# Square sums two heads behind the queries, squares rounded straight from the bank, and weight remainders shared by GpSimd and VectorE in the stage between two layers

## The reference

```python
x = x + softmax(q k / scale) v @ Wo                      # end of layer 0's attention
x = x + einsum('btd,rde->bte', layernorm(x), factors) / sqrt(8) + bias
q = (layernorm(x) @ Wq).reshape(B, Sq, 16, 128)          # layer 1
q = q * rsqrt(mean(square(q), axis=-1) + 1e-5) * gq
```

## Time and profile before

| | us |
|---|---|
| median of three runs | 2167.49 (2165.17 to 2168.35) |
| profiled execution | 2165.27 |
| its span | 2163.5 |
| TensorE busy in the span | 2098.3 (97%) |
| VectorE, ScalarE, GpSimd busy | 1622.5, 1085.9, 1425.9 |
| granted TensorE clock, mean | 0.994 of full speed |

### The profile page before, as it was taken

One profiled execution on the slowest core, in us unless ns is written; L12 is line 12 of the kernel. 1 busy time (PEld: TensorE's weight loads), 2 busy tenths in 40 slices (PEclk: granted clock), 3 DMA queues, 4 the chain that ended last, 5 costly groups with the idle time before them and its releaser, 6 DMA issues. The chain is left out here.

```text
span 2163.5 us, 27510 instructions
## 1 busy us (share of the span) xinstructions
PE 2098.3 (97%) x8514; PEld 1522.0 (70%) x8514; DVE 1622.5 (75%) x2560; ACT 1085.9 (50%) x3408; POOL 1425.9 (66%) x1071
## 2 busy tenths in 40 slices
PE   7999999999999999999999888999999999999999
PEld 7777777777677777777777456666666666665998
DVE  4889999999999999999987642556566666652577
ACT  3565556555555565655656137444434344431433
POOL 1477787777877887778776146187878778771221
PEclk9999999999999999999999999999999999999999
DMA  3000000000000000000010410011011111101110
GB/s 132 29 15 19 26 29 16 29 15 29 29 15 15 29 29 15 22 23 29 21 43 1 147 40 1 29 43 58 29 57 38 49 53 33 43 1 52 37 52 25
DMA packets 15140, 75.64 MB, mean 35 GB/s; under 512 B 1746, under 2 KB 2114, under 8 KB 13986
## 3 DMA queue, kind: packets, MB, share of 16 engines
q1 hardware_dynamic: 14994, 73.89, 10.4%
HBM read 72.97 MB, written 0.92 MB: 34 GB/s over the span
## 5 line engine op out<-in xcount | busy, mean ns | idle before, releaser
L539 ACT ACTIVATE l_prod_act<-l_prod_act 125x128 f32<-125x128 f32 x1152 | 342.1, 299 | 354.6 <-DVE l_prod_act L714 354.5
L634 POOL TENSOR_TENSOR l_prod<-l_prod 125x256 f32<-125x256 f32 x480 | 350.3, 738 | 239.5 <-DVE l_prod L714 239.5
L968 POOL TENSOR_TENSOR l_acc<-l_acc,l_probs 125x896 f32<-125x896 f32 x160 | 346.2, 2163 | 81.5 <-ACT l_probs L918 65.8
L714 DVE TENSOR_TENSOR l_prod<-l_side,xq 125x512 f32<-125x512 f32 x480 | 324.8, 677 | 45.0 <-PE l_side L823 38.4
L988 DVE TENSOR_TENSOR l_scaled<-l_slots,rk 125x896 f32<-125x896 f32 x192 | 206.9, 1084 | 197.6 <-PE l_slots L1053 197.5
L918 ACT ACTIVATE l_probs<-l_scaled 125x896 f32<-125x896 f32 x192 | 182.9, 953 | 320.5 <-DVE l_scaled L988 298.8
L628 POOL TENSOR_TENSOR l_acc<-l_acc,l_probs 125x896 f32<-125x896 f32 x160 | 339.3, 2121 | 0.0
L557 ACT ACTIVATE l_probs<-l_slots,mask_bias 125x448 f32<-125x448 f32 x384 | 225.0, 623 | 59.8 <-PE l_slots L775 54.1
L684 DVE SCALAR_TENSOR_TENSOR top<-l_side,mask_bias,top 125x448 f32<-125x448 f32 x330 | 216.5, 664 | 7.9 <-PE l_side L806 7.9
L539 ACT ACTIVATION_READ_ACCUMULATOR l_prod_act<-l_prod_act 125x1 f32 x1152 | 217.0, 188 | 0.0
L723 DVE TENSOR_REDUCE l_msq<-l_prod 125x4 f32<-125x256 f32 x480 | 196.3, 410 | 22.4 <-POOL l_prod L634 22.4
(11 more groups left out here) (256 smaller groups left out, 4623.8 us busy)
## 6 DMA issues: line engine op xcount, KB each, us to landing
land<-in_ctxT SPq DMA_DIRECT2D x32, 750.0 KB, 4.0
l_nat<-in_ctxN SPq DMA_DIRECT2D x16, 750.0 KB
post_we<-in_experts SPq DMA_DIRECT2D x20, 384.0 KB, 3.0
spare<-in_ctxN SPq DMA_DIRECT2D x8, 750.0 KB
nat<-in_ctxN SPq DMA_DIRECT2D x8, 750.0 KB
spare<-in_wo SPq DMA_DIRECT2D x2, 2048.0 KB, 8.7
spare<-in_wqT SPq DMA_DIRECT2D x4, 512.0 KB, 9.2
mid_fac<-in_factors SPq DMA_DIRECT2D x1, 2048.0 KB, 8.0
```

What stands on the lines that cost most here:

```text
L539: last = act.activation(whole, whole, ACT.Copy, accum_out=msq[:, t, 4 * g + c:4 * g + c + 1])
L634: pool.tensor_tensor(buf[:, :, 0:C // 2], buf[:, :, 0:C // 2], buf[:, :, C // 2:C], ALU.add).then_inc(s.half_sum, 1)
L714: dve.tensor_tensor(to[:, :, :], bank, xt.unsqueeze(1).to_broadcast([KT, 4, C]), ALU.mult).then_inc(s.side_dve, 1)
L968: pool.tensor_tensor(acc[:, :], acc[:, :], P[t % NP][:, :], ALU.add).then_inc(s.acc, 1)
```

## The change

Four things are changed in `between_layers`.

1. `ms` of head n stands two heads behind the query product, with the last two sums of half 0 among the first queries of half 1; `sqh` and `sql` have three buffers.
2. ScalarE computes the rounded square from the bank a second time, with a rounded output, instead of rounding `sq`. The even heads' copies of half 0 go from ScalarE to VectorE, which copies after both squares.
3. Weight remainders of even n stay with GpSimd, those of odd n are VectorE's, with a semaphore of their own. GpSimd's bias add is done tile by tile, those of half 1 between the first four heads' squares.
4. The reciprocals of half 0 stand at heads 2 to 5 of half 1 on VectorE, and ScalarE's rounding of the inverse at head 6 instead of head 2.

```diff
...
 MID += [("t1", 0, 0), ("t1", 0, 1), ("f", 0, 0), ("f", 0, 1), ("y", 1, 1), ("t2", 0, 0), ("t2", 0, 1), ("o", 1, 0), ("o", 1, 1)]
-for h in range(H + 1):
-    MID += [("q", 0, h)] if h < H else []
-    MID += [("ms", 0, h - 1)] if h >= 1 else []
+for h in range(H):
+    MID += [("q", 0, h)]
+    MID += [("ms", 0, h - 2)] if h >= 2 else []
     MID += [("t1", 1, 0), ("t1", 1, 1), ("f", 1, 0), ("f", 1, 1)] if h == 5 else []
...
     MID += [("q", 1, h)] if h < H else []
-    MID += [("ms", 1, h - 1)] if 1 <= h <= H else []
+    MID += [("ms", 0, H - 2 + h)] if h < 2 else []
+    MID += [("ms", 1, h - 2)] if 2 <= h < H + 2 else []
     MID += [("r", 0, h - 9)] if 9 <= h < H + 9 else []
...
 for h in range(H + 1):
...
     if kind == "q":
-        return "dve" if half == 0 and i % 2 else "act"
+        return "dve" if half == 0 else "act"
     return {"y": "act", "t1": "act", "k": "act", "o": "dve", "f": "dve", "r": "dve", "t2": "dve"}.get(kind)
...
     s1 = semaphores(sem, tag + "1", LN_SEMAPHORES)
...
     s = semaphores(sem, tag, ["ld_fac", "ld_bias", "ld_wq", "ld_wk", "ld_g", "ld_next", "ready", "on_act", "on_dve", "fac", "gain",
-                 "zero", "one_r", "bias", "rk_std", "rk_inv", "x_hi", "w_hi", "w_lo", "sq", "sq_hi", "sq_lo", "ms", "std", "rinv", "r_hi", "r_lo"])
+                 "zero", "one_r", "bias", "rk_std", "rk_inv", "x_hi", "w_hi", "w_lo", "w_lo1", "sq", "sq_hi", "sq_lo", "ms", "std", "rinv", "r_hi", "r_lo"])
     with ExitStack() as ctx:
...
         bk = [ctx.enter_context(nc.psum_tensor(f"{tag}_bk{i}", [128, 512], F32)) for i in range(8)]
...
         ident_r = sb("ident_r", [128, 128], F32R)
...
         sq = [sb(f"sq{i}", [HD, HALF], F32) for i in range(2)]
-        sqh = [sb(f"sqh{i}", [HD, HALF], F32R) for i in range(2)]
-        sql = [sb(f"sql{i}", [HD, HALF], F32R) for i in range(2)]
+        sqh = [sb(f"sqh{i}", [HD, HALF], F32R) for i in range(3)]
+        sql = [sb(f"sql{i}", [HD, HALF], F32R) for i in range(3)]
         std = [sb(f"std{i}", [H, HALF], F32) for i in range(2)]
...
         rlo = [sb(f"rlo{i}", [128, HALF], F32R) for i in range(2)]
...
-                need(pool, s.ms, n - 1)
+                need(pool, s.ms, n - 2)
+                pool.wait_ge(s.sq, n + 1)
                 pool.wait_ge(s.sq_hi, n + 1)
-                pool.tensor_tensor(sql[n % 2][:, :], sq[n % 2][:, :], sqh[n % 2][:, :].bitcast(F32), ALU.subtract).then_inc(s.sq_lo, 1)
-
-            def add_bias(half):
-
-                pool.wait_ge(s1.xn, 4 * half + 4)
-                four = m.x[:, 4 * half:4 * half + 4, :]
-                pool.tensor_tensor(four, four, bias[:, :].unsqueeze(1).to_broadcast([TT, 4, D]), ALU.add).then_inc(s.bias, 1)
-
-            add_bias(0)
-            for n in range(NWQ - 1):
+                pool.tensor_tensor(sql[n % 3][:, :], sq[n % 2][:, :], sqh[n % 3][:, :].bitcast(F32), ALU.subtract).then_inc(s.sq_lo, 1)
+
+            def add_bias(j):
+
+                pool.wait_ge(s1.xn, j // 4 * 4 + 4)
+                pool.tensor_tensor(m.x[:, j, :], m.x[:, j, :], bias[:, :], ALU.add).then_inc(s.bias, 1)
+
+            for j in range(4):
+                add_bias(j)
+            for n in range(0, NWQ - 1, 2):
                 weights_low(n)
             for n in range(2 * H):
-                if n == 3:
-                    add_bias(1)
                 square_low(n)
-                if n + NWQ - 1 < 2 * H:
+                if n % 2 == 1 and n + NWQ - 1 < 2 * H:
                     weights_low(n + NWQ - 1)
+                if n < 4:
+                    add_bias(4 + n)
...
         def _(act):
...
                 if job == ("y", 1, 0):
...
                         weights_high(n)
-                if job == ("q", 1, 2):
+                if job == ("q", 1, 6):
                     round_inverse(0)
...
                     round_inverse(1)
...
                 elif kind == "q":
...
                     need(act, s.sq_lo, n - 1)
-                    act.activation(sq[i % 2][:, :], bank[:, 0:HALF], ACT.Square).then_inc(s.sq, 1)
+                    act.activation(sq[n % 2][:, :], bank[:, 0:HALF], ACT.Square).then_inc(s.sq, 1)
+                    need(act, s.ms, n - 2)
+                    act.activation(sqh[n % 3][:, :], bank[:, 0:HALF], ACT.Square).then_inc(s.sq_hi, 1)
                     if taken_by(job) == "act":
                         act.activation(qs_of(half, i), wide(bank), ACT.Copy).then_inc(s.on_act, 1)
-                    act.wait_ge(s.sq, n + 1)
-                    need(act, s.ms, n - 1)
-                    act.activation(sqh[i % 2][:, :], sq[i % 2][:, :], ACT.Copy).then_inc(s.sq_hi, 1)
                     if n + NWQ - 1 < 2 * H:
...
                 else:
...
                 dve.wait_ge(s.r_hi, half + 1)
...
                 dve.tensor_tensor(rlo[half][0:H, :], std[half][:, :], rhi[half][0:H, :].bitcast(F32), ALU.subtract).then_inc(s.r_lo, 1)
+
+            def weights_low(n):
+
+                need(dve, s.ready, RING.index(("q", (n - NWQ) // H, (n - NWQ) % H)) + 1 if n >= NWQ else 0)
+                dve.wait_ge(s.w_hi, n + 1)
+                dve.tensor_tensor(wql[n % NWQ][:, :, :], wq[:, :, HD * (n % H):HD * (n % H) + HD], wqh[n % NWQ][:, :, :].bitcast(F32),
+                                  ALU.subtract).then_inc(s.w_lo1, 1)
...
             dve.tensor_reduce(fsum[:, :, :], fac[:, :, :, :].rearrange("p k r d -> p k d r"), AX.X, ALU.add).then_inc(s.fac, 1)
...
             dve.wait_ge(s.rk_std, 1)
...
                 dve.reciprocal(m.rk[:, i, :, :], m.rk[:, i, :, :]).then_inc(s.rk_inv, 1)
+            for n in range(1, NWQ - 1, 2):
+                weights_low(n)
             for job in RING:
                 kind, half, i = job
+                if kind == "q" and half == 1 and 2 <= i < 6:
+                    invert(0, i - 2)
+                if kind == "q" and i % 2 == 0 and H * half + i + NWQ - 1 < 2 * H:
+                    weights_low(H * half + i + NWQ - 1)
                 if taken_by(job) != "dve":
...
                 if job == ("r", 0, 0):
-                    for part in range(4):
-                        invert(0, part)
                     inverse_low(0)
...
                 if kind == "r" and half == 0 and 10 <= i < 14:
...
                         dve.wait_ge(s.on_dve, taken(job))
...
                 elif kind == "f":
-                    dve.wait_ge(s.bias, half + 1)
+                    dve.wait_ge(s.bias, 4 * half + 4)
                     two = m.x[:, 4 * half + 2 * i:4 * half + 2 * i + 2, :]
...
                                              ALU.mult, ALU.add).then_inc(s.on_dve, 1)
...
                     dve.tensor_tensor(xlo[:, i, HALF * half:HALF * half + HALF], bank[:, 0:HALF],
...
                 elif kind == "q":
-                    dve.wait_ge(s.sq, H * half + i + 1)
+                    dve.wait_ge(s.sq_hi, H * half + i + 1)
                     dve.tensor_copy(qs_of(half, i), wide(bank)).then_inc(s.on_dve, 1)
...
                     need(dve, s.ready, RING.index(("k", half, i - 2)) + 1 if i >= 2 else 0)
...
                     if half == 1 and i == 0:
...
                     one = one_r[:, H - 1 - i:H - 1 - i + 128]
-                    pe.matmul(bk[7][:, 0:HALF], one, sql[i % 2][:, :], start=i == 0, stop=False)
-                    pe.matmul(bk[7][:, 0:HALF], one, sqh[i % 2][:, :], start=False, stop=i == H - 1).then_inc(s.ms, 1)
+                    at = (H * half + i) % 3
+                    pe.matmul(bk[7][:, 0:HALF], one, sql[at][:, :], start=i == 0, stop=False)
+                    pe.matmul(bk[7][:, 0:HALF], one, sqh[at][:, :], start=False, stop=i == H - 1).then_inc(s.ms, 1)
                     continue
...
                 bank = bk[n % NRING]
...
                     old = RING[n - NRING]
...
                     if old[0] == "q":
-                        pe.wait_ge(s.sq, H * old[1] + old[2] + 1)
+                        pe.wait_ge(s.sq_hi, H * old[1] + old[2] + 1)
                 if kind in ("y", "ya"):
...
                     for h in heads:
...
                 elif kind == "q":
...
                     n = H * half + i
-                    pe.wait_ge(s.w_lo, n + 1)
+                    pe.wait_ge((s.w_lo, s.w_lo1)[n % 2], n // 2 + 1)
                     for kc in range(KC):
```

## The result

The changed kernel takes 2153.25 us (median, 2152.15 to 2154.89) against 2166.33 before in the same measurement; the ratio is 0.9945 (0.9933 to 0.9957), 11.9 us less (9.3 to 14.5); the two medians lie 13.1 apart. The prediction's sum was 2152.7. The profiled execution took 2154.89, span 2153.1, so 10.4 less than the one before.

What follows compares the result with a forecast made beforehand. TensorE was held by a round trip through ScalarE and GpSimd for square remainders between the layers. Savings of 3.6 + 0 + 10.9 + 0.3 = 14.8 us gave 2150.5 by the profiled execution, 2152.7 as median; range 2147 to 2159.

Steps and rivals of the forecast that it cites:

- What bounds it: Between the layers, TensorE's square sums wait for GpSimd's square remainders, a round trip: 16 times, 17.0 us.
- part 1: Squares two heads behind, three buffers: the remainder gets 3.26 us to arrive before its sum.
- Part 2: Rounding from the bank: chain about 2.2 us, square taken as 0.54, ScalarE's period in half 1 1.62 a head.
- Part 3: Shared weight remainders: GpSimd 3.17 us in two heads, under TensorE's 3.26; VectorE's block 0.35 alone, up to 1.5.
- Step 4, A: First query matmul to head 6 of half 0: TensorE stands 3.4 us before head 3's sum; 3.6 saved.
- Step 5, B: Head 6 to head 11: 2.4 us lost at head 9, 0.8 for the clock; 12.1 against 12.10, nothing gained.
- Step 6, C: Head 11 to first spread-out inverse r(0,0): 27.4 against 38.33 us, 10.9 saved; waits 0.7 (inverse rounding), 1.7 (r(0,0)).
- Step 7, D: First spread-out inverse to last square sum: 0.40 more for a later sum, 1.08 idle goes; 0.3 us saved.
- Sum: Whole kernel: 3.6 + 0 + 10.9 + 0.3 = 14.8 us saved, 2152.7 us as median; chance 0.61.
- third rival: TensorE's wait moves from the squares to the weight remainders, 2.3 us a head, time 2163.5; chance 0.06.
- Signs: Profile after: sums hardly wait after head 11, two heads take 3.26 to 3.4 us, GpSimd over 90% busy there.
- the three places: Waits for VectorE's remainders: 2 to 4 us before queries of heads 3 and 9, 1 to 3 before r(0,0).

Runs made afterwards that it cites:

- e1: Kernel before with only the sums two heads behind, three buffers and ScalarE's inverse rounding at head 6 of half 1: 2149.26 us, ratio 0.9929.
- e3: Changed kernel with the sums one head behind again, three buffers kept: 2163.45 us, ratio 0.9995.
- e4: Changed kernel with the rounded square taken from the full square in memory again, behind a wait: 2156.82 us, ratio 0.9961.
- e2: Changed kernel with all weight remainders on GpSimd: 2152.97 us, ratio 0.9947.
- e8: Changed kernel, weight remainders of heads 3 and 9 on GpSimd, half 1's bias adds two heads later, inverse's remainder before head 11's weight remainder: 2149.80 us, ratio 0.9922.
- e5: Changed kernel with head 9's weight remainder of half 0 on GpSimd: 2150.77 us, ratio 0.9927.
- e11: Changed kernel, all weight remainders on GpSimd, which waits before the squares of head 7 of half 1 for VectorE's inverse remainder: 2147.20 us, ratio 0.9915.
- e7: Changed kernel with head 3's weight remainder on GpSimd and half 1's bias adds two heads later: 2153.55 us, ratio 0.9945.
- e9: Changed kernel, no VectorE weight remainders before head 13, half 1's bias adds two heads later, inverse's remainder before head 11's weight remainder: 2143.47 us, ratio 0.9898.

## Why the prediction was right, point by point

- **What bounds it, part 1.** Right, and shown by e1 and e3: the distance alone (with the rounding of the inverse moved to suit it) takes 16.5 us off the stage, everything else without it 2.3.
- **Part 2.** The prices are right: the square from the bank with a rounded output lasts 0.54, and ScalarE's period in half 1 is 1.63. What the part gained by itself stays open. e4's period of 1.84, which costs 1.4 in C, is that of a rounding right behind the square with a wait; the kernel before had the copy between the two and a period of 1.62.
- **Part 3.** GpSimd's two heads stayed under TensorE's 3.26, and less was lost on GpSimd than assumed: its weight blocks last 0.74 in the median, 0.91 at most, its square blocks 1.16 in the median, 1.60 at most. But the price for VectorE was seen as one block at most. Sixteen of its blocks:

```profile
L1349 DVE TENSOR_TENSOR mid_wql<-mid_fac,mid_wqh x16: 360/773/1629, 1238.0 to 1335.5; 128x256 fp32r<-128x256 f32 x16
```

  The shortest is 0.36, the longest 1.63, just over the bound of 1.5, yet e2, e4 and e8 show 8.93, 3.75 and 2.54. That one engine holds the other off for whole instructions (the 0.48 behind the last block), and that a waiting one is not next in line, are two things; only the first was in the sum. The share, where it stands in the changed kernel, cost more than it gave: e5 takes one of VectorE's blocks away and B is 2.87 shorter; e11 takes all away and makes the gap, and the stage is 6.5 shorter, in the time 0.9915 for 0.9945.
- **Step 4, A.** 19.5 predicted, 19.45 measured; the wait 3.4 and 2.91. The low clock is in the measured value and cost nothing beside GpSimd's time, as said. That the sum meets to 0.05 is luck: sum 3 started 13.5 us after the first query and not 14.1, since GpSimd's first bias add did not wait for VectorE's weight block, and the transposes and f matmuls took 5.46 as before, not 0.4 less.
- **Step 5, B.** The term that was mis-sized: 12.1 predicted, 13.93 measured. TensorE waited 3.11 and not 2.4, because the four normalisations took 3.01 us and not 1.9, and the clock fell in full (nine matmuls at 0.37), where half of that was put in.
- **Step 6, C.** 27.4 and 27.88; the wait at r(0,0) 1.7 and 2.07. The other single wait stood elsewhere: 0.76 before the first sum of half 1, for ScalarE's root to have read bank 7, which the prediction had not seen; ScalarE itself waited only 0.20 for the reciprocal, for which 0.7 was put in.
- **Step 7, D.** 0.3 and 0.08: the low clock behind r(0,0), which cost 1.5 (D is 19.68 in e5, with the same wait and the full clock), wasn't in it.
- **Sum.** 14.8 predicted, 12.35 in the stage, 10.4 between the two profiled executions, 11.9 by the ratio. That 2152.7 lies 0.5 from 2153.25 is partly luck: the median of before was 1.2 lower this time, and the saving smaller than forecast by 1.7 to 2.9, whichever measure of it is taken. The third rival's 2163.5 leaves 1.2 us for the rest of A without a reason; with the 3.6 of step 4 it would be about 2161.
- **Signs.** The sums' waits went, the three places are there, and two heads in C take 3.34 (27.88 less the waits, over 7.5). GpSimd is busy 23.09 of 27.88 us in C, 83% and not over 90%: with the 2.8 us of waits taken out it is 92%.

## What to carry to other kernels

When an engine waits in every round for a result that goes over two others, put more independent work between the two ends before making the way shorter or sharing it: one more head and one more buffer gave 16.5 us of the stage, and with the rest added it was 12.35. Before work goes from a full engine to an idle one, look at what stands in front of it in that engine's list (here two normalisations that wait for a third engine) and whether the two hold each other off. Look also at how a wait would end: in e2 it ended only because the engine that waited had starved the others. A wait removed has to be followed to the next one by the timeline, not added up.

## What the runs showed of the hardware

- A VectorE subtraction with two inputs in memory can be held off by GpSimd's subtractions and additions not for one block but for as long as they follow each other: 8.93 us (e2) and 3.60 (e11) for one that lasts 0.61 alone, 3.75 (e4) and 2.54 (e8) for one that lasts 0.36. It isn't always so: in e1 the same instruction as in e2 got in behind one block (1.33 us), and in e7 the same as in e8 (1.27). What decides between the two was not tried.
- Four normalisations on VectorE, with one tensor from memory, are slowed by GpSimd too, but not by a whole block each: 1.38 us alone, 2.63 (e7), 3.01 (the changed kernel) and 4.08 (e8) beside GpSimd.
- A wait does not have a fixed clock price. Behind 2.07 us the clock fell in the changed kernel and not in e5 (2.06). At one place in A it fell behind 2.84 us in e11 and not in e2, whose program is the same up to there; in e9 it fell behind 0.83 and 0.99. What takes TensorE from 2.4 to 1.2 GHz at one time and not at another stays open.
